# A five-layer graph kernel on one NeuronCore: four quads of adjacency tiles counted as sums instead of three

## The reference

```python
# block 0: only the last 100 neighbours of a row count, halved for each neighbour behind
rank = jnp.cumsum(adj != 0, axis=1); deg = rank[:, -1:]
k = jnp.minimum(deg, 100.0); pos = rank - (deg - k)
w = mask * jnp.where(pos > 0, 0.5 ** (k - pos), 0.0)
x = layernorm(x + w @ (x @ weight) + bias)
# block 1: two gated layers, each m = adj @ (h @ W), then sigmoid/tanh gates with h
# block 2: degree-normalised adj @ x @ W;  block 3: neighbour mean and own row times W.T
x = layernorm(x + block(x, adj))
```

## Time and profile before

| | us |
|---|---|
| median of 3 runs (lowest, highest) | 436.82 (436.73, 436.91) |
| the profiled execution's own time | 436.67 |
| its span, first to last instruction | 434.6 |
| PE busy | 411.6 (95%) |
| DVE busy | 297.2 (68%) |
| ACT busy | 205.7 (47%) |
| POOL busy | 115.6 (27%) |

### The profile page before, as it was taken

How to read it: one execution, slowest core, us unless ns; L and a number is a source line. 1 busy time by engine, 2 the same in 40 slices (tenths; PEclk the granted TensorE clock), 3 DMA queues, 4 the chain that set the end, 5 groups by cost and what they waited for, 6 DMA issues and landing times.

```text
span 434.6 us, 6527 instructions
## 1 busy us (share of the span) xinstructions
PE 411.6 (95%) x2332; PEld 195.4 (45%) x2332; DVE 297.2 (68%) x855; ACT 205.7 (47%) x333; POOL 115.6 (27%) x154
## 2 busy tenths in 40 slices
PE   7678998999999999999999999999999999999991
PEld 2223332334334434445655555555544454454480
DVE  3468849758965997455954666886948757477773
ACT  3356787877787877417734443533322122112100
POOL 9211314211420100042221304334424434401111
PEclk9989999999999999999999999999999999999997
DMA  8999999999999992451110200000000101200000
GB/s 111 106 160 109 106 108 108 106 108 107 108 107 107 108 108 21 98 63 26 24 21 16 27 12 2 0 2 0 2 0 14 24 14 24 27 12 26 23 22 18
DMA packets 25103, 23.74 MB, mean 55 GB/s; under 512 B 14536, under 2 KB 16488, under 8 KB 25072
## 3 DMA queue, kind: packets, MB, share of 16 engines
q0 software_dynamic: 9360, 16.78, 38.6%
q1 hardware_dynamic: 15424, 6.36, 7.3%
q10 hardware_dynamic: 288, 0.20, 0.2%
HBM read 69.45 MB, written 1.06 MB: 162 GB/s over the span
## 4 chain that ended last, share of the span: by engine, by line
PE 74%; DMA 16%; DVE 3%; POOL 3%; issue 2%; ACT 0%; POOLq 0%
PE Y L1060 45%; DMA adjT<-in_adjT 16%; PE both L966 11%; PE Y L945 5%; PE Y L957 3%; PE both L927 2%; PE both L924 2%; PE both L973 2%; POOL adjT L311 1%; POOL rstd L283 1%; PE both L931 1%; PE both L918 1%; PE Y L1066 0%; DVE stat L505 0%; DVE work L509 0%
## 5 line engine op out<-in xcount | busy, mean ns | idle before, releaser
L1060 PE MATMUL Y<-adjT,S 128*128 128x512 fp8e4 (+1 forms) x1056 | 231.9, 373 | 0.1
L1060 PEld LDWEIGHTS Y<-adjT,S 128*128 128x128 f16 x1056 | 101.5, 98 | 109.3 <-POOL S L298 1.2
L396 ACT ACTIVATE wgt<-both,consts 128x512 int16<-128x512 f32 x128 | 85.4, 687 | 32.4 <-PE both L966 28.7
L283 POOL TENSOR_TENSOR rstd<-stat,mhalf 128x4 f32<-128x4 f32 (+2 forms) x29 | 36.1, 1245 | 157.7 <-DVE stat L511 157.7
L966 PE MATMUL both<-adjT,fix 128*128 128x512 fp8e4 x160 | 61.8, 386 | 7.1 <-DMA adjT<-in_adjT 6.1
L945 PE MATMUL Y<-wgt,S 128*128 128x512 bf16 x160 | 61.2, 383 | 0.0
L966 PE MATMUL both<-adjT,tri 128*128 128x512 fp8e4 x160 | 61.2, 382 | 0.0
L311 POOL DMA_DIRECT2D adjT<-in_adjT x63 | 35.6, 577 | 74.7 <-DMA adjT<-in_adjT 74.7
L531 DVE SCALAR_TENSOR_TENSOR work<-Y,yT 64x512 f32<-64x512 f32 x30 | 20.8, 694 | 50.7 <-ACT yT L355 50.3
L355 ACT ACTIVATE yT<-Y 64x512 f32<-64x512 f32 x30 | 17.6, 586 | 75.0 <-PE Y L1060 50.2
L966 PEld LDWEIGHTS both<-adjT,fix 128*128 128x128 bf16 x160 | 15.5, 97 | 50.6 <-ACT wgt L396 29.4
(11 more groups left out here) (120 smaller groups left out, 438.6 us busy)
## 6 DMA issues: line engine op xcount, KB each, us to landing
adjT<-in_adjT POOLq DMA_DIRECT2D x63, 256.0 KB, 39.0
out_rows<-xrow SPq DMA_DIRECT2D x7, 128.0 KB, 1.9
xrow<-in_xrow SPq DMA_DIRECT2D x1, 640.0 KB, 9.1
x<-in_w_gates SPq DMA_DIRECT2D x1, 512.0 KB, 5.4
biases<-in_biases SPq DMA_DIRECT2D x1, 384.0 KB, 4.2
x<-S SPq DMA_TRANSPOSE x24, 2.4
xrow<-in_xrow SPq DMA_DIRECT2D x1, 256.0 KB, 4.4
adjT<-in_adjT POOLq DMA_DIRECT2D x2, 128.0 KB, 6.1
```

Source lines behind the costliest of these rows:

```text
L283: nc.gpsimd.tensor_tensor(rstd[:, 0:blocks], stat[:, 2, 0:blocks], mhalf[:, 0:blocks], ALU.pow)\
L396: nc.scalar.activation(wgt[:, c, tiles % 2, :], V[c][:, :], ACT.Relu, **({"bias": tile_bias[sums]} if sums else {})).then_inc(w_ready[c], 1)
L1060: mm = nc.tensor.matmul(bank(layer, g)[:, 0:nb * P], S[layer % 2][:, jb, :], cols[:, jb, :], start=(jb == 0), stop=(jb == JB - 1), skip_gr ...
```

## The change

`MASKED` becomes (7, 5, 3, 1): a block has 4 quads and 16 tiles, 20 steps, and begins with a quad. The quads' sums have the same code. The opening products with `cutw` are gone (the constant goes into ACT's biases, one more column of `consts`), and the first count product starts the accumulation. The closing `fix` product is gone: the degree is picked from `V` with tile 0's row 0 added in, by DVE for both halves. The pairs of tiles arrive in straight order. The layer-0 sums move from Y[0], Y[1] to Y[3] and half of the bank `both` (`own`), so layer 1's groups 0, 1 and 2 can be done early for tiles 0 to 23: 72 products, 11 of them behind the last block. `layer1` then starts with 24 products of group 3 where 32 of groups 2 and 3 stood. The table `BETWEEN` has 16 products with constants in block 0 (before: 18) and 7 ahead of block 1 (before: none).

```diff
-MASKED = (6, 4, 2)
+MASKED = (7, 5, 3, 1)
+        own = [Y[3][:, :], gates[0][:, 0:2, :].rearrange("p b d -> p (b d)")]
-            return Y[(layer * G + g + 2) % 4] if layer else Y[g % 2]
+            return Y[(layer * G + g) % 4]
-                act.wait_ge(v_total[0], q + 1)
-                nc.scalar.activation(deg_row[0][0:1, :], V[0][0:1, :], ACT.Copy).then_inc(deg_picked[0], 1)
             def pick_degree(q, c):
-                dve.wait_ge(v_total[c], q + 1)
+                dve.wait_ge(w_ready[c], (q + 1) * NS)
-                nc.vector.tensor_copy(deg_row[c][0:1, :], V[c][0:1, :]).then_inc(deg_picked[c], 1)
+                nc.vector.scalar_tensor_tensor(out=deg_row[c][0:1, :], in0=adj_tile(q, 0, c)[0:1, :], scalar=-float(KEEP + STEP),
+                                               in1=V[c][0:1, :], op0=ALU.mult, op1=ALU.add).then_inc(deg_picked[c], 1)
...
             convert(7)
             convert(6)
+            sum_quad(0, 7)
+            spread(0, 7)
+            mask_quad(0, 7)
             convert(5)
-            sum_quad(0, 6)
-            spread(0, 6)
-            mask_quad(0, 6)
-            sum_quad(0, 4)
+            sum_quad(0, 5)
             convert(4)
+            spread(0, 5)
+            mask_quad(0, 5)
             convert(3)
             convert(2)
+            sum_quad(0, 3)
...
-            sum_quad(2, 6)
-            sum_quad(2, 4)
-            spread(2, 6)
+            sum_quad(2, 5)
+            spread(2, 7)
+            mask_quad(2, 7)
             rows0(1, False)
-            mask_quad(2, 6)
+            sum_quad(2, 3)
             rows0_out(1)
             split_rows0(1)
-            spread(2, 4)
-            sum_quad(2, 2)
-            mask_quad(2, 4)
-            spread(2, 2)
-            mask_quad(2, 2)
+            spread(2, 5)
+            mask_quad(2, 5)
+            sum_quad(2, 1)
+            spread(2, 3)
+            mask_quad(2, 3)
+            spread(2, 1)
+            mask_quad(2, 1)
+            sum_quad(3, 7)
+            pick_degree(2, 0)
             pick_degree(2, 1)
             take_y(0, 4)
             take_y(0, 5)
...
                             if s == 0:
                                 if q >= 1:
+                                    pe.wait_ge(w_ready[c], q * NS)
                                     pe.wait_ge(deg_picked[c], q)
-                                nc.tensor.matmul(V[c][:, :], cutw[:, :], ones[:, :], start=True, stop=False,
-                                                 skip_group_check=True)
-                            count(q, c, s, 0).then_inc(v_done[c], 1)
+                            count(q, c, s, 0, start=(s == 0)).then_inc(v_done[c], 1)
...
                         pe.wait_ge(w_ready[c], (q + 1) * NS)
-                        count(q, c, NS - 1, 1, stop=True).then_inc(v_total[c], 1)
                         weigh(q, 0, c)
...
                 combine(0, 6)
                 combine(0, 7)
-                product(1, 2, 0, 24)
-                product(1, 3, 0, 8)
+                product(1, 3, 0, 24)
                 gate_sums()
                 product(1, 0, 24, 32)
                 product(1, 1, 24, 31)
                 open_gates()
                 product(1, 1, 31, 32)
                 product(1, 2, 24, 32)
-                product(1, 3, 8, 25)
+                product(1, 3, 24, 32)
+                product(1, 4, 0, 9)
                 combine(1, 0)
```

More of the change, by code:

```diff
@@ L132, in build @@
         quad_bias = [consts[:, 3 * P + i:3 * P + i + 1] for i in range(NM)]
-        tile_bias = [None] + [consts[:, 3 * P + NM + i:3 * P + NM + i + 1] for i in range(NM)]
+        tile_bias = [consts[:, 3 * P + NM + i:3 * P + NM + i + 1] for i in range(NM + 1)]
         Y = [ps(f"Y{c}", [P, GC]) for c in range(4)]
@@ L386, in _ @@
                         act.wait_ge(v_done[c], q * NS + s + 1)
-                        if q == 0 and s == STEPS.index(("quad", MASKED[0])) and c == 0:
+                        if q == 0 and s == 0 and c == 0:
                             act.wait_ge(consts_in, 16)
@@ L395, in _ @@
                         else:
-                            nc.scalar.activation(wgt[:, c, tiles % 2, :], V[c][:, :], ACT.Relu,
-                                                 **({"bias": tile_bias[sums]} if sums else {})).then_inc(w_ready[c], 1)
+                            nc.scalar.activation(wgt[:, c, tiles % 2, :], V[c][:, :], ACT.Relu, bias=tile_bias[sums]).then_inc(w_ready[c], 1)
                     tiles += kind == "tile"
-                act.wait_ge(v_total[0], q + 1)
-                if q >= 1:
-                    act.wait_ge(row_out[0], 16 * q)
-                nc.scalar.activation(deg_row[0][0:1, :], V[0][0:1, :], ACT.Copy).then_inc(deg_picked[0], 1)
                 take_y(0, 2 * q)
@@ L721, in _ @@
             output_weights()
[L722 to L726, removed]
+            spread(0, 3)
+            mask_quad(0, 3)
+            sum_quad(0, 1)
+            spread(0, 1)
+            mask_quad(0, 1)
             add_bias()
+            sum_quad(1, 7)
+            pick_degree(0, 0)
             pick_degree(0, 1)
@@ L937, in _, with opens_sum @@
             TILES = [jb for kind, jb in STEPS if kind == "tile"]
+            summing = set()
+            def opens_sum(q, c):
+                if (q, c) in summing:
+                    return False
+                summing.add((q, c))
+                if q >= 1:
+                    pe.wait_ge(y0_out[c], q)
+                return True
             def weigh(q, jb, c):
-                if jb == JB - 1 and q >= 1:
-                    pe.wait_ge(y0_out[c], q)
+                first = opens_sum(q, c)
                 if q == 0 and jb % B == B - 1:
                     pe.wait_ge(s_ready, G - jb // B)
-                mm = nc.tensor.matmul(Y[c][:, :], S[0][:, jb, :], wgt[:, c, TILES.index(jb) % 2, :].bitcast(BF16),
-                                      start=(jb == JB - 1), stop=(jb == 0), skip_group_check=True)
+                mm = nc.tensor.matmul(own[c], S[0][:, jb, :], wgt[:, c, TILES.index(jb) % 2, :].bitcast(BF16),
+                                      start=first, stop=(jb == 0), skip_group_check=True)
                 if jb == 0:
@@ L956, in weigh_masked, with count @@
                         pe.wait_ge(s_ready, G - quad)
-                mm = nc.tensor.matmul(Y[c][:, :], S[0][:, quad * B + k, :], wq[:, k, c * GC:(c + 1) * GC].bitcast(BF16),
-                                      start=False, stop=False, skip_group_check=True)
+                mm = nc.tensor.matmul(own[c], S[0][:, quad * B + k, :], wq[:, k, c * GC:(c + 1) * GC].bitcast(BF16),
+                                      start=opens_sum(q, c), stop=False, skip_group_check=True)
                 if c == 1:
                     mm.then_inc(masked_used, 1)
-            def count(q, c, s, which, stop=False):
+            def count(q, c, s, which, start=False):
                 kind, at = STEPS[s]
                 if kind == "tile":
-                    return nc.tensor.matmul(V[c][:, :], (tri, fix)[which][:, :], adj_tile(q, at, c), start=False, stop=stop,
-                                            skip_group_check=True)
+                    return nc.tensor.matmul(V[c][:, :], (tri, fix)[which][:, :], adj_tile(q, at, c), start=start,
+                                            stop=(which == 0 and s == NS - 1), skip_group_check=True)
                 e = q * NM + MASKED.index(at)
@@ L1048, in product @@
                 if first == 0:
-                    if layer == 1 and 2 <= g < 4:
-                        pe.wait_ge(y0_out[g - 2], Q)
+                    if layer == 1 and g == 3:
+                        pe.wait_ge(y0_out[0], Q)
                     elif layer > 1 or g >= 4:
```

105 lines of the change are left out of this document (56 added, 49 removed), and 18 rows, old and new, of tables (BETWEEN, ORDER).

## The result

The changed kernel took 443.91 us (median of 4 runs, 443.27 to 445.94) beside 436.77 for the kernel before: ratio 1.0172, 95% interval 1.0137 to 1.0206, so 7.1 us slower. The forecast was 438.2, with a range up to 440.0. The direction was right and the size was not. The profiled execution is the slowest of the four, 445.94 us with a span of 443.9; in the other three the granted clock was a little higher (0.972 to 0.984 against 0.968).

A forecast was written before the change was run, and what follows sets the result against it. PE bounds the old kernel at 40.3 us a block; changed, DVE at 40.9 paces layer 0. PE resumes 4.95 us later, then saves 3.45: +1.5 on 436.67 gives 438.2, range 434.3 to 440.0.

The forecast's parts named there:

- The counted work: Whole kernel: 59 x 0.216 = 12.7 us less PE work; in layer 0 DVE needs 40.9 us a block.
- rival (a): End of layer 0: the clock stays high, PE resumes 3.5 us later and saves 3.45: 436.7, no change; chance 0.20.
- PE (... 36 to 37) falls behind neither: Layer 0's blocks: PE's 36 to 37 us stay under DVE's 40.9 and the transfers' 39.3, so DVE sets the pace.
- The forecast's own signs of being wrong: Blocks 2 and 3: wrong if DVE waits for transfers or PE is still unbroken there; no size given.
- The forecast's 1.5 us: Whole kernel: PE resumes 4.95 us later behind layer 0, then saves 3.45: +1.5 us on 436.67.
- At the two block changes before, the same fall costs nothing: Block changes before layer 0's end: a clock fall is hidden, as DVE's sum, picks and `take_y` take 3.8 us meanwhile.
- the last combine's share: End of layer 0: about 7 of 15 products run at half speed, 1.5 us; bounds 0 and 3.2.
- Rival (d): Blocks: PE's masked products delay a count, or the pick is slow; 0.5 to 0.8 us a block, about 440; chance 0.13.
- Rival (b): Blocks 1 to 3: DVE keeps transfers' pace, under 39.3 us: 432.5 to 434; chance 0.18 together with a half-way 435.6.
- The semaphore: DVE's spreads: 1.89 us when the waiting mask is next; the skill's free semaphore would give 1.67, result about 435.6.
- The busiest engine: Whole kernel: easing PE, the engine with the highest occupancy, brings all 12.7 us: 424; chance 0.04.

## Why the prediction was right in direction and wrong in size

**The counted work: right.** 59 x 0.216 less on PE, a block of 40.9 us for DVE: in the kernel with the second buffer, where no spread waits, blocks 2 and 3 take 40.8 and 39.4 from pick to pick (101.62, 142.39, 181.76; block 3 has no sum of a next block, 1.4, in it). Its last mask is written at 181.9, forecast 182.2, its last combine begins at 185.15, forecast 185.4, PE resumes at 193.65, and the kernel takes 436.7. That is rival (a), clock up and nothing else lost, to a tenth of a microsecond; though (a) had the clock stay up through four gaps at the end, and here PE came later and had three. Quad 1's spread, sums, root wait and picks all have the durations that were read from the earlier trace rows. (One reading of the earlier trace rows is off: PE's unbroken 9s begin with the eighth slice, not the seventh. Nothing hangs on it.)

**"PE (... 36 to 37) falls behind neither": the step that failed.** It compared sums of work per block, as if both engines ran a block in parallel. With one buffer of masks, DVE can't begin quad 1's spread before PE has used quad 3's, and PE, in its queue's order, can't begin the next block before it has quad 1's last weights from DVE. What counts is the sum: PE from first count to quad 3's k = 1 product, 33.4, DVE's spread and mask, 6.8, PE's 11 products to the next first count, 2.4: 42.65 us where the forecast had 40.9. In its terms, PE's last tile step was to end 1.3 us behind mask 3; it ended 3.5 us behind (183.6 against 180.1). The warning stood in the rows: the spread at 127.17 waits 3.29 us for a masked product, the largest of five such waits in the old trace, 10.3 us in all. They were read as VectorE's spare time, since it was busy for 30.63 of 40.30, and the new sum took VectorE's work without asking what TensorE had to do first in each of those places. Price in the profiled execution: 5.83 us of waits; with the clock held it is the difference of the ratios with constants, 1.0109 - 1.0017, or about 4 us. The forecast's own signs of being wrong, waits for transfers or an unbroken PE in blocks 2 and 3, did not cover this: neither came.

**The direction was right in part by luck.** The forecast's 1.5 us came from a clock that falls at the end of layer 0. With the engines as parallel as it took them to be and the clock up, the kernel is exactly as fast as the one before (ratio 1.0000 with the second buffer). What made the changed kernel slower is for the most part what the forecast had left out.

**"At the two block changes before, the same fall costs nothing": wrong as well, and smaller.** It would hold if the first count waited for DVE's picks with time to spare. But quad 1's products, the weighing ones and seven early products stand in PE's queue ahead of the first count and end behind the picks, and at the lower clock they ended 1.3 us later at block 2. (At block 3 the clock stayed up.) Together with the last combine's share, forecast at 1.5, the clock was worth 2.5 us by medians. In the profiled execution these terms account for nearly all of the 7.8 us missed (445.94 against 438.17): 5.83 of waits, 0.44 for a later transfer (63.83 against 63.39), 0.97 between last mask and last combine (188.63 to 194.30 = 5.67 against 4.7; more products ran at the lower clock), 0.2 from combine to resuming, 0.2 behind it. Of the 5.83, some is the clock's, as the late first count makes the next wait longer (4.6 with the clock held).

**Rival (d)** named the place, "PE, held in its queue by masked products", but saw it in late counts and priced it at 0.5 to 0.8 us a block. It came at a spread's buffer, and at 1.0, 3.0 and 1.8 us in blocks 1 to 3 (95.28; 130.14 and 139.25; 181.89).

**Rival (b)**, 432.5 to 434, was put down to VectorE keeping pace with the transfers. Its number came with three edits that the change doesn't have (buffer, gaps, order): 433.1. Its condition did not quite: block 2 takes 39.85 us there from pick to pick, still above the transfers' 39.3.

**The semaphore.** A spread whose mask waits for it costs 1.89 (139.25 to 141.14), as the sum had it. The Trainium skill, "VectorE: DVE Perf Modes", section "The DRAIN you can't avoid", would give 1.67; the traces before and after differ from it by the same 0.22, and the distance stayed in every block.

**The busiest engine.** TensorE has the highest occupancy in both kernels, 95% and 92%, and taking work from one engine alone gave little: 16 products fewer, 3.5 us, brought 0.8 (three quads without opening and closing products), and VectorE's shorter order brought nothing. The Trainium skill, "Perfetto Trace Analysis", section "Optimization Strategy", adds that a gap repeating on the engine that should be saturated can mean too few buffers. This trace shows such a gap, though on VectorE: 1.01, 2.38 and 1.80 us in blocks 1 to 3, each in front of quad 1's spread, and one more buffer took it away.

## What to carry to other kernels

Before two engines' work per period is compared as if it ran in parallel, go through every wait that hands a buffer back, and ask where the two waits of a ring meet: if A's last part needs B's buffer back and B's next period needs A's last part, the two parts add up, and the busy shares don't show it. A change that makes the last unit of a period longer (here a quad where single tiles stood) moves that ring onto the path even where total work falls. Name the instruction that each part of the ring really ends with: here it was the last weights and not the picks, and a reordering that delayed the weights by 1.2 us gained nothing, although it saved VectorE time. Try the second buffer before the order of instructions: the same reordering was worth nothing with one buffer and 3.6 us with two.

## What the runs showed of the hardware that was not expected

TensorE's clock fell although no single gap was long: at the end of layer 0 the gaps are 1.56, 0.60 and 0.48 us, with two products between, and the clock went to 0.67 in 186 to 188. But the gaps don't tell whether it falls. At the end of block 1 they are 1.55, 0.60, 0.60 and 0.49 us, and it fell to 0.84 in 100 to 102 and 0.50 after; at the end of block 2 they are 1.56, 0.60, 0.60 and 0.53, and it stayed at 1.00. No run here shows what made the difference. The changed kernel's times are spread over 2.7 us in four executions; kernels whose trace has the clock at 1.00 over layer 0's block ends are spread over 0.2 us (four executions, constants in the gaps) to 1.0 (eleven, second buffer and products in the gaps). That the falls differ from one execution to the next is a likely reason, but only one execution of each kernel has a trace.
